# A four-bank PSUM ring for the scan's input u, multiplied in place, with exp(dt*A) written in place in SBUF

## What is computed

```
xp = layernorm(x) @ w_xproj ; dt_in, Bs, Cs = split(xp)
delta = softplus(dt_in @ w_dt + b_dt);  A = -exp(A_log)
for each token t:
    h = exp(delta[t] * A) * h + (delta[t] * xn[t]) * Bs[t]
    y[t] = sum over the 64 states of h * Cs[t]
```

## Time and profile before

| | |
|---|---|
| median of 3 runs | 1220.89 us (1219.04 to 1223.19) |
| profiled execution, own time | 1217.73 us |
| its span | 1215.9 us |
| DVE busy | 1074.0 us, 88% |
| PE busy (matmul) | 902.4 us, 74% |
| POOL busy | 815.2 us, 67% |
| ACT busy | 809.6 us, 67% |
| TensorE clock granted, mean | 0.84 |

### The profile page before, as it was taken

One profiled execution on the slowest core, in us unless ns is written; L12 is line 12 of the kernel. 1 busy time (PEld: TensorE's weight loads), 2 busy tenths in 40 slices (PEclk: granted clock), 3 DMA queues, 4 the chain that ended last, 5 costly groups with the idle time before them and its releaser, 6 DMA issues. The chain is left out here.

```text
span 1215.9 us, 19663 instructions
## 1 busy us (share of the span) xinstructions
PE 902.4 (74%) x4292; PEld 366.9 (30%) x4292; DVE 1074.0 (88%) x2434; ACT 809.6 (67%) x2199; POOL 815.2 (67%) x558
## 2 busy tenths in 40 slices
PE   4276778787788766887678776777778776787875
PEld 1022332333333232332223333233233322333332
DVE  4389989989899988999899998899989998999993
ACT  4277764878648765577657876477864877656772
POOL 6466765867567766677667676586766777667663
PEclk9558988879887888879888898788988888897887
DMA  4544356543584344644456335553358434574440
GB/s 118 124 130 122 117 132 144 151 113 91 132 200 127 117 112 118 169 130 117 114 139 157 114 119 130 146 144 117 90 133 200 127 117 104 128 181 138 119 117 9
DMA packets 124123, 155.29 MB, mean 128 GB/s; under 512 B 32722, under 2 KB 57062, under 8 KB 124006
## 3 DMA queue, kind: packets, MB, share of 16 engines
q1 hardware_dynamic: 123494, 153.74, 47.6%
q0 software_dynamic: 512, 0.27, 0.2%
HBM read 137.63 MB, written 4.52 MB: 117 GB/s over the span
## 5 line engine op out<-in xcount | busy, mean ns | idle before, releaser
L1338 POOL TENSOR_TENSOR prod<-hst,C 128x1024 f32<-128x1024 f32 x256 | 603.4, 2357 | 340.5 <-DVE hst L1151 340.5
L1151 DVE TENSOR_TENSOR_SCAN hst<-bank,dbx 128x512 f32<-128x512 f32 x512 | 618.8, 1210 | 35.4 <-ACT bank L626 35.4
L626 ACT ACTIVATE bank<-wide,A_rep 128x512 f32<-128x512 f32 x512 | 351.6, 687 | 319.7 <-DVE hst L1151 221.7
L1145 DVE TENSOR_TENSOR dbx<-bank,B 128x512 f32<-128x512 f32 x512 | 342.7, 670 | 56.0 <-PE bank L871 46.4
L871 PE MATMUL bank<-spread,sel_bc 96*128 96x512 bf16 x512 | 218.1, 441 | 66.3 <-DVE dbx L1145 47.0
L640 ACT ACTIVATE prob<-s_sb,nmax 128x96 f32<-128x96 f32 x512 | 183.9, 360 | 0.0
L892 PE MATMUL bank<-prod,sel_red 128*32 128x512 f32 x1024 | 164.1, 718 | 4.3 <-POOL prod L1338 4.3
L902 PE MATMUL bank<-k,q 128*128 128x384 f32 x256 | 137.8, 626 | 30.4 <-DVE nmax L1164 19.1
L909 PE MATMUL bank<-ident,prob 128*96 128x128 f32 x512 | 92.2, 311 | 61.9 <-ACT ao L656 61.6
L871 PEld LDWEIGHTS bank<-spread,sel_bc 96*128 96x128 bf16 x512 | 55.0, 108 | 219.9 <-DVE dbx L1145 146.5
L1343 POOL TENSOR_TENSOR prob<-prob,pinv 128x384 f32<-128x384 f32 x128 | 106.1, 829 | 8.8 <-DVE pinv L1172 6.3
(11 more groups left out here) (180 smaller groups left out, 926.5 us busy)
## 6 DMA issues: line engine op xcount, KB each, us to landing
wide<-dt_rows SPq DMA_DIRECT2D x512, 256.0 KB, 4.5
vw<-v_tok SPq DMA_DIRECT2D x80, 64.0 KB, 3.0
spread<-parts SPq DMA_DIRECT2D x96, 32.0 KB, 1.9
x_sb<-in_L_attn_x_dram SPq DMA_DIRECT2D x8, 256.0 KB, 4.6
dt_rows<-sp_t SPq DMA_DIRECT2D x8, 256.0 KB, 4.5
out_dram<-outb SPq DMA_DIRECT2D x8, 256.0 KB, 2.2
q<-qn SPq DMA_DIRECT2D x112, 16.0 KB
vw<-v_tok SPq DMA_DIRECT2D x16, 48.0 KB, 2.6
```

The lines of the kernel that those rows point to most:

```text
L626: nc.scalar.activation(daP[s % 2][:, :], wide[m % SLOTS][:, s % 2, :], ACT.Exp, scale=A_rep[:, g:g + 1]).then_inc(exp_done, 1)
L1145: v.tensor_tensor(dbx[:, s % 3, :], uP[s % 2][:, :], B2[p][:, :], ALU.mult).then_inc(dbx_done, 1)
L1151: v.tensor_tensor_scan(hst[:, s % 4, :], daP[s % 2][:, :], dbx[:, s % 3, :], 0.0, ALU.mult, ALU.add).then_inc(scan_done, 1)
L1338: g.tensor_tensor(prod[:, 2 * (m % 4):2 * (m % 4) + 2, :], hst[:, 2 * (m % 2):2 * (m % 2) + 2, :], C2[p][:, :].unsqueeze(1).to_broadcast([ ...
```

## The change

The two banks of da and the two of u become one ring of four banks for u. The exponential is written over its own input in the `wide` slot. DVE multiplies u by B in place in the bank and the scan reads da from SBUF and u*B from the bank. The ring `dbx` is gone. The matmul and the exponential are now issued three units ahead instead of one. `unit_u` of unit s waits for the scan of unit s-4; the exponential waits for its transfer alone; `widen` of pair m waits for the two scans of pair m-4.

```diff
-AHEAD = 1
+AHEAD, U_AHEAD = 3, 3
...
-        daP, uP, yP, sP, ptP, jobP = bank[0:2], bank[2:4], bank[4], bank[5], bank[6], bank[7]
+        uP, yP, sP, ptP, jobP = bank[0:4], bank[4], bank[5], bank[6], bank[7]
...
-        dbx = sb("dbx", [128, 3, L])
...
-                wait(sp, exp_done, B * UNITS + 2 * (m - SLOTS) + 2)
+                wait(sp, scan_done, B * UNITS + 2 * (m - SLOTS) + 2)
...
-                wait(act, scan_done, B * UNITS + s - 1)
...
-                nc.scalar.activation(daP[s % 2][:, :], wide[m % SLOTS][:, s % 2, :], ACT.Exp,
+                nc.scalar.activation(wide[m % SLOTS][:, s % 2, :], wide[m % SLOTS][:, s % 2, :], ACT.Exp,
...
-                wait(pe, dbx_done, B * UNITS + s - 1)
-                mm(uP[s % 2][:, :], sel_bc[:, i, :, :].rearrange("k j n -> k (j n)"), spread[p][:, q, :],
+                wait(pe, scan_done, B * UNITS + s - 3)
+                mm(uP[q][:, :], sel_bc[:, i, :, :].rearrange("k j n -> k (j n)"), spread[p][:, q, :],
...
-                    if s < UNITS - 1:
-                        unit_u(B, p, s + 1)
+                    if s + U_AHEAD < UNITS:
+                        unit_u(B, p, s + U_AHEAD)
                     elif not last(B):
-                        unit_u(B + 1, 1 - p, 0)
+                        unit_u(B + 1, 1 - p, s + U_AHEAD - UNITS)
...
-                wait(dve, scan_done, B * UNITS + (s - 2 if s else 0))
-                v.tensor_tensor(dbx[:, s % 3, :], uP[s % 2][:, :], B2[p][:, :], ALU.mult).then_inc(dbx_done, 1)
+                v.tensor_tensor(uP[s % 4][:, :], uP[s % 4][:, :], B2[p][:, :], ALU.mult).then_inc(dbx_done, 1)
...
-                v.tensor_tensor_scan(hst[:, s % 4, :], daP[s % 2][:, :], dbx[:, s % 3, :], 0.0, ALU.mult,
+                v.tensor_tensor_scan(hst[:, s % 4, :], wide[(s // 2) % SLOTS][:, s % 2, :], uP[s % 4][:, :], 0.0, ALU.mult,
```

More of the change, by code:

```diff
@@ L878, in front @@
                     pre_job(name, B, p, front=True)
-                unit_u(B, p, 0)
+                for s in range(U_AHEAD):
+                    unit_u(B, p, s)
             def y_start(B, p):
```

## The result

The changed kernel takes **1366.9 us** (median; 1366.1 to 1368.5), the kernel before 1220.5. The ratio is 1.119, with a 95% interval from 1.116 to 1.121: slower by 146 us. The forecast was 1284, in a range up to 1325. The sign was right, and the loss is over twice the 63 us of the sum.

What follows compares the result with a forecast made beforehand. DVE was taken to bound the kernel at 1.71 us a unit, leaving only idle time to gain. Costs of 93 us less a gain of 30 gave +63: 1281, or 1284 us on the median, range 1240 to 1325.

Steps and rivals of the forecast that it cites:

- items 0 and 7: First and last items: item 0 was to cost 7.5 us and item 7, which prepares nothing, 6.3 us.
- The two transfer chains: Transfers of pairs 24 and 31: costs of 3.3 and 2.7 us an item; as the only costs, 1238 us, chance 0.17.
- What bounds the kernel: DVE, busy 1074 of 1216 us: a unit costs it 1.71 us, which the change doesn't shorten; only idle time is gained.
- Gain, -30 us: DVE's waits for u: 30 of them, 30.0 us beyond the start, all taken away by issuing the matmul sooner.
- Cost 1, the gate: PE's first matmul of a slot waits 2.8 us later, delaying jobs DVE needs: 5.2 us an item, between 2.5 and 8.
- cost 4: Seam between items: ACT's late v copy delays PE's projection and first scores, 1.5 us; loop turns 1.5 more each, twice.
- The output job of slot 22: Feed-forward result of slot 21, taken in slot 22, late behind PE and two ACT copies: 1.5 us, by likeness to es1.
- Cost 2, pair 24: ACT stands at pair 24's transfer in slot 45, delaying es2's sum and es3: 3.3 us an item, from 2 to 4.5.
- Cost 3, pair 31: Pair 31's transfers behind q's sixteen come later, scan 62 waits 6.0 us instead of 3.32: 2.7 an item, 1.5 to 3.
- What was put at nothing: Exponential's time and write to SBUF, scan's operands, and multiply writing a bank (20 ns either way): taken as 0.
- The rival of the same bank: DVE's multiply slows reading and writing one bank: up to 276 us, 1560; small form 50 ns, 1310. Chance 0.12.
- The condition that would have made the kernel faster: If ACT's stand at pair 24 in slot 45 is under 1 us, only the 30 us go: 1191, chance 0.07.

Runs made afterwards that it cites:

- e1: The changed kernel with the matmul of u issued two units ahead instead of three: 1287.4 us, ratio 1.055.
- e9: The changed kernel with only SP's transfers reordered, the blocks of parts of u and of q spread out: 1275.4 us, ratio 1.046.
- e10: The changed kernel with SP's transfers spread and the matmul of u two units ahead instead of three: 1195.7 us, ratio 0.978.
- e16: The changed kernel with the u matmul repeated once more at the end of each PE slot: 1372.4 us, ratio 1.125.
- e8: The changed kernel with the u matmul repeated three more times at the end of each PE slot: 1384.1 us, ratio 1.134.
- e3: The changed kernel with the exponential one unit ahead instead of three, u still three ahead: 1327.7 us, ratio 1.088.
- e2: The changed kernel with the matmul of u issued one unit ahead instead of three: 1302.1 us, ratio 1.066.
- e17: The kernel before with only the exponential written in place in SBUF, so the scan reads both operands from SBUF: 1558.9 us, ratio 1.279.

## Why the prediction was right in sign and wrong in size

Three steps failed: the gain was taken whole, the gate's jobs were priced at the higher level of PE's clock with two of them missing, and the seam and items 0 and 7 were put too low. The two transfer chains held.

**What bounds the kernel, right.** The unit still costs DVE 1.71 us: the in-place multiply to its scan is 0.58 us, and the scan to the next multiply 1.12. In the timeline of the changed kernel, item 3 (slots 3 and 4):

```profile
552.76 0.67 DVE L1143 TENSOR_TENSOR bank<-bank,B 128x512 f32<-128x512 f32 x1
553.34 1.21 DVE L1149 TENSOR_TENSOR_SCAN hst<-wide,bank 128x512 f32<-128x512 f32 x1
554.46 0.67 DVE L1143 TENSOR_TENSOR bank<-bank,B 128x512 f32<-128x512 f32 x1
```

**Gain, -30 us: too high.** The waits for u did go: all but the 7.7 us at the start. But they were paid back. A gain of 30 us is 3.75 an item. Where the waits stood most, units 20 to 32, the changed kernel is 0.6 us an item slower than before, and even e1, with less of the gate, gains only 1.1 there and 1.5 in all of 4 to 46. The step "I take the whole" failed. A wait that is removed is a gain only up to the next thing that is late, and I looked for that only at the two waits of the start.

**Cost 1, the gate, 5.2 us an item: measured at least 9.8** (162.7 - 152.9, after against e1; with the transfers spread, e9 against e10, it is 9.9). It is a lower bound, since e1 moves the gate back by 1.71 of the 2.8 us. The mechanism was right and was the largest cost. The terms against the waits of DVE in item 2 of the changed kernel:

```profile
387.24 0.70 DVE L1143 TENSOR_TENSOR bank<-bank,B 128x512 f32<-128x512 f32 x1 [3.69 <-PE bank L869]
395.01 0.70 DVE L1143 TENSOR_TENSOR bank<-bank,B 128x512 f32<-128x512 f32 x1 [1.56 <-PE bank L901]
401.33 0.70 DVE L1143 TENSOR_TENSOR bank<-bank,B 128x512 f32<-128x512 f32 x1 [0.30 <-PE bank L901]
407.65 0.70 DVE L1143 TENSOR_TENSOR bank<-bank,B 128x512 f32<-128x512 f32 x1 [0.30 <-PE bank L901]
431.31 0.70 DVE L1143 TENSOR_TENSOR bank<-bank,B 128x512 f32<-128x512 f32 x1 [2.22 <-PE bank L901]
442.83 0.70 DVE L1143 TENSOR_TENSOR bank<-bank,B 128x512 f32<-128x512 f32 x1 [2.53 <-PE bank L901]
487.61 0.70 DVE L1143 TENSOR_TENSOR bank<-bank,B 128x512 f32<-128x512 f32 x1 [0.84 <-PE bank L901]
```

Slot 5 was forecast at 1.4 and is 1.56; slots 8 and 11 at 0.25 and are 0.30. Slots 21 and 25 were forecast at 0.3 and 0.4 and are 2.22 and 2.53. Slot 44, with 0.84, was not in the list. The first row is the wait for the scores of block 0, of cost 4. The difference is in PE's timeline of item 2, ahead of slot 5 (first group of rows) and ahead of slot 21 (second):

```profile
391.80 0.39 PE L869 MATMUL bank<-spread,sel_bc 96*128 96x512 bf16 x1 [1.44 <-DVE hst L1149]
392.12 1.07 PE L891 MATMUL bank<-prod,sel_red 128*32 128x512 f32 x8
393.12 1.13 PE L953 MATMUL bank<-mprobT,dec_m 128*128 128x512 f32 x2
394.08 0.81 PE L901 MATMUL bank<-k,q 128*128 128x384 f32 x2
...
427.37 0.39 PE L869 MATMUL bank<-spread,sel_bc 96*128 96x512 bf16 x1 [1.68 <-DVE hst L1149]
427.69 1.91 PE L891 MATMUL bank<-prod,sel_red 128*32 128x512 f32 x8
429.53 1.65 PE L901 MATMUL bank<-k,q 128*128 128x384 f32 x2
```

From the gate to the end of the scores, slot 5 took 394.08 + 0.81 - 391.80 = 3.1 us, and I had 2.98. Slot 21 took 429.53 + 1.65 - 427.37 = 3.8, and I had 2.0. The same reduction ran in 1.07 us in the one place and in 1.91 in the other: the two levels of PE's clock (granted 1.00 from 387.5 to 395.0 us, 0.51 from 427.7 to 431.1). The kernel before had already run slot 19 at the lower level (granted 0.51), as the rows of its item 2 show:

```profile
379.89 1.90 PE L892 MATMUL bank<-prod,sel_red 128*32 128x512 f32 x8
381.71 1.65 PE L902 MATMUL bank<-k,q 128*128 128x384 f32 x2
```

So slot 21 could have been priced from the trace of before: these two jobs at 1.90 and 1.65 us, where the sum had 0.99 and 0.81, add 1.75 to its 0.3, and 2.22 was measured. Slot 23, whose two jobs take 1.06 and 0.91 us in item 2 before and 1.94 and 1.65 after, fell to the lower level only with the change. In item 3 slot 5 is at the lower level too (reduction 1.94, scores 1.49) and DVE waits 4.23 us instead of 1.56. So **the step that failed took every duration from one stretch, that runs at the higher level**, and applied it to all slots. I had named the lower level for the range (8 us) and still fell short, because the list of victims was short too: there is no term for the maximum of es0 (0.3 to 1.3 us in every item) nor for slot 44 (0.84 in most). es1 was forecast at 1.1 and is 1.25 in five items and 2.9 in three. The output job of slot 22 went the other way: I had it at 1.5 by likeness, and it is 0.5 (13.0 less the 9.6 of the end, in seven items).

How much of the 9.8 the clock carries stays open. Behind its stand of 1.68 us at the gate PE worked at the lower level in slot 19, and behind one of 1.44 us at the higher in slot 3. e16 and e8 raise the clock only by giving PE more work. They show that the clock alone is not the way out.

**Cost 2, pair 24, 3.3 us an item: measured 4.3** (stretch 46-53). The wait is where it was put and as long as it was said, "about 7 us in seven items" (50.7 us in 7):

```profile
500.97 0.72 ACT L624 ACTIVATE wide<-wide,A_rep 128x512 f32<-128x512 f32 x1 [9.30 <-DMA wide<-dt_rows]
503.26 0.16 DVE L1179 RECIPROCAL minv<-msum 128x1 f32<-128x1 f32 x1 [7.33 <-ACT mprob L662]
509.12 0.69 DVE L1175 TENSOR_REDUCE mmx<-bank 128x1 f32<-128x512 f32 x1 [1.30 <-PE bank L932]
```

ACT stands 9.30 us at pair 24's transfer where it stood 4.81, and the sum of es2 comes 2.3 us after it, as worked out. The 1.0 us that is missing is the last row: I let the 1.33 us wait for es3 go up in the new wait, and it stayed. e3 shows the cause, ACT's lead: with a lead of one, this stretch is back at 18.9.

**Cost 3, pair 31, 2.7 us an item: about right.** Units 53 to 64 took 2.6 us longer. The wait at scan 62 is not 6 us but 3.2, because part of the lateness already shows as a new wait of 1.94 us ahead of it (softmax reciprocal, 10.7 us in 7). In e1 that wait is gone, the exponential's are 38.5 us instead of 27.1, and the stretch is the same 26.2: it is no cost beside this one. Both rows are of item 2:

```profile
522.86 0.18 DVE L1170 RECIPROCAL pinv<-psum_r 128x4 f32<-128x4 f32 x1 [1.94 <-ACT prob L638]
538.78 2.33 DVE L1149 TENSOR_TENSOR_SCAN hst<-wide,bank 128x512 f32<-128x512 f32 x2 [3.17 <-ACT wide L624]
```

**Cost 4, the seam, 1.5 us an item: too low.** Units 0 to 4 took 5.5 us longer. Of these 2.4 go with one unit less of lead (after against e1), mostly the wait at slot 5, and 3.1 are left in e1. The row at 387.24 above is the other part: DVE's wait for the scores of block 0, 3.69 us in slot 2. They end at 387.02, 7.75 us after the start of scan 63 in the changed kernel, and 3.12 us after it before: 4.6 us later, where I had 0.5 to 2.5. Ahead of them PE had stood 5.81 us for ACT's copy of the attention's probabilities, not for v's, and its reduction ran in 1.94:

```profile
378.55 0.65 PE L916 MATMUL bank<-probT,vw 96*32 96x128 f32 x8 [5.81 <-ACT probT L647]
...
381.64 1.94 PE L891 MATMUL bank<-prod,sel_red 128*32 128x512 f32 x8
```

The term as written, all of it from ACT's lead, is not what the runs show. DVE's wait in slot 2, as a mean over items 1 to 6, is 3.3 us. It falls to 2.1 with the exponential one unit ahead (e3), to 2.6 with the transfers spread (e9), and to 1.2 with u one unit ahead (e2), where PE stood even longer for that copy (10.9 us). So ACT's lead is one part of it, and PE's gate another, by these numbers no smaller. No run takes the two fully apart, and the rest stays open.

**Items 0 and 7: far too low.** Together they cost 34.5 us (19.5 + 15.0) where the sum had 13.8. With their share of the gain, 7.5, the sum had only 6.3. Item 7 prepares nothing, so that its loss is nearly all the gate's: e1 gives back 12.6 of the 15.0. For item 0 the sum had, of the gate, only es1 and slot 23 (0.4, the wait at slot 25); DVE also waited there 2.90 us at slot 8 and 2.37 at slot 21.

**What was put at nothing.** The exponential into SBUF takes 713 ns against 687, covered as said. The Trainium skill, page "ScalarE: Activation LUTs", section "Step-by-step: what each stage is for", says that a write to PSUM is faster than one to SBUF; the two groups agree, by 26 ns. The multiply's mean is 683 against 670, inside the 20 ns. Those that follow no wait grew as well, from 668 to 681, so the write into the bank may cost these 13 ns (7 us over 512); from multiply to scan it is still 0.58. The rival of the same bank falls, in its large form and in the small one of 50 ns.

**The sum, again.** An item costs 18.8 us more, in table terms: one unit of the gate 9.8, pair 24 4.7, pair 31 2.6, the seam that is left in e1 3.1, less 1.5 of gain in the rest (rounded differences of the table, all but the first of e1 to before; e1's part of the gate is in them). I had 5.2, 3.3, 2.7 and 1.5 less 3.75. Six items are 113 us, items 0 and 7 34.5; together 147. Of the 84 us between 63 and 147, the gate's terms with the clock and the missing victims are 28 in the six items, the gain that did not come 14, the seam 10, pair 24 8, and items 0 and 7 with the loop's ends the rest. The condition that would have made the kernel faster, ACT under 1 us at pair 24, was far off; and even with both faults mended the ring reaches 1182, and the kernel before with the same order of transfers 1174.

## What to carry to other kernels

A longer ring that is freed by a later consumer moves the producer's wait, and an in-order engine holds every job behind it: cost what stands behind the wait, and put the wait behind the job that the critical engine wants next (68 us here). Price each such job at the clock level of its own stretch, since the same reduction took 1.07 us in one slot here and 1.91 in another. And look at the order of the transfers before the depth of buffers: a block of twelve and one of sixteen transfers in one queue cost the kernel before 46 us and the ring 92.

## What the runs showed of the hardware that I had not expected

**A scan with both operands in SBUF does not run beside GpSimd's SBUF work.** Its mean went from 1210 ns to 1966 (e17), and the time from 1218 to 1559 us, though the scan alone still takes 1.21. One operand in a bank, either one, avoids it: before (exp in the bank) and after (u in the bank) both have 1209 to 1210. The Trainium skill, page "SBUF — State Buffer", section "SBUF: two separate sides", says so: a VectorE operation with two SBUF inputs and a GpSimd operation that reads SBUF use one shared port pair as an exclusive lock for the whole instruction, and the loser blocks. The rows of e17 agree (3.02 us beside the product, ending 1.1 us after it). So the two halves of this change depend on each other: the exponential could go to SBUF only because u stays in its bank for the scan.

**More work can raise PE's clock and not the speed.** Three more matmuls a slot took the mean granted clock from 0.797 to 0.913, and the kernel from 1366.9 to 1384.1 us.
